# One load a stack from rows kept by row tile, and the first unit's maxima and shift in halves of its heads

## The chip, the cores and the metric

The kernel runs on one NeuronCore of a Trainium2 chip. Five engines work from their own instruction queues and meet at semaphores: TensorE (PE, matmuls), VectorE (DVE), ScalarE (ACT), GpSimd (POOL) and SyncE (SP, which only issues DMAs). The metric is the time of one execution on the device in microseconds (us).

## What is computed

Two layers over eight sequences of 512 tokens with 128 channels: an attention with 16 heads of 8 channels and a sliding window of 128 keys, then a block of causal attention and a top-2 mixture of eight experts. Each is followed by a residual sum and a layer norm.

```python
def attention(x, w_qkv, allowed):            # both layers, heads of 8 channels
    q, k, v = split(x @ w_qkv)               # [B, H, T, 8]
    scores = einsum('bhtd,bhsd->bhts', q, k) * 8 ** -0.5
    attn = softmax(where(allowed, scores, -inf))
    return merge(einsum('bhts,bhsd->bhtd', attn, v)) @ w_out

x = layernorm(x + attention(x, ..., (j <= i) & (j >= i - 128)))
h = layernorm(x, g1, b1)
r = x + attention(h, ..., j <= i)
f = layernorm(r, g2, b2)
out = sum over the two best experts e of gate_e * (gelu(f @ w1[e] + b1[e]) @ w2[e] + b2[e])
x = layernorm(x + out + r)
```

## The kernel before

**Units and iterations.** The attention work is cut into 16 units: unit u below 8 is sequence u in the local layer, unit 8 + b is sequence b in the causal layer. The main loop runs over iterations `it` from -2 to 15, each a row of steps k (6 in iteration -2, 14 for a local unit, 20 for a causal one). In iteration `it` the scores of unit `it` are made while the maxima of the units after it, the products with v of this one, and the last stages of the one before run beside them. Every engine walks through the same steps in a fixed order written out by hand (`MAXIMA`, `JOBS`, `project_at`); no planner moves anything. A queue that waits for a semaphore holds back all that stands behind it on its engine.

**Stacks.** The scores must be accurate although bf16 matmuls make them. So `project(u)` makes q and k in float32 in PSUM, and three bf16 parts are split off: the high part (`high_part`, L772, ScalarE), the rest (`split_rest`, L934, VectorE), the middle part (`middle_part`, L780, ScalarE) and the low part (`low_part`, L942, VectorE). SP stores these parts to a scratch in DRAM (`store`, L460), each into as many slots as it has factors in the product (three, two and one), and loads them back in another order (`load`, L467) as a stack: for each of two row tiles of 64 partitions, 48 rows of contraction (six slots of 8 channels), 8 heads and 512 tokens, so that one matmul over 48 rows sums all partial products. Row 48 and 49 of each half hold ones for k (`L447`, loaded once) and the shift for q (`load_shift`, L489).

**Maxima and shift.** Before the exponential the kernel needs a shift a query. `maxima(u, m)` (L1381) makes masked scores of 14 pieces of a local unit (20 of a causal one) on TensorE, L1402 the masks and L1411 the products; `maximum(u, m)` (L898, local L907 and L911) reduces each piece on VectorE. `split_shift` (L924) splits the negated maxima into two bf16 numbers, `turn_shift` (L1520) transposes them on TensorE, `take_shift` (L817) copies them on ScalarE, and `load_shift` puts them into rows 48 and 49 of q's stack by DMA. Then `scores(u, k)` (L1365) gives scores less the maximum in one matmul, and `exponent` (L737) takes the exponential.

**Order at the start.** Iteration -2 projects units 0 and 1. SP stores and loads unit 0, waits until that stack has landed (L475, since there is one scratch), then stores and loads unit 1. The maxima of unit 0 take steps 0 to 10 of iteration -1, the values job (`values`, L1481) stands at its step 1, and its shift follows; those of unit 1 begin at step 11 of iteration -1 and run on through steps 0 to 10 of iteration 0, one a step; unit 2's begin at step 11 of iteration 0. Unit 2 is projected at step 0 of iteration 0. PSUM buffers for scores, maxima, projections and turns come from a ring of three (`RING_AT`): each entry waits for the third one before it to be read.

## Time and profile before

| | |
|---|---|
| median of three runs | 786.75 us (780.80 to 787.21) |
| the profiled execution | 787.42 us, of which the span is 785.7 us |
| TensorE / VectorE / ScalarE / GpSimd busy | 81% / 73% / 59% / 54% of the span |
| first matmul of the maxima | 25.57 us |
| first score | 45.39 us |
| first score of unit 1 | 75.60 us |
| moved by DMA | 82.22 MB in 57549 packets |

A busy share is an average over stages with different limits: what a change in one stage is worth is read from the stage, not from the share. Starts are counted from the beginning of the span. "Landing" is when the data of a DMA is there and its semaphore is up; SP's row shows only the issue. The granted clock is TensorE's, as a share of 2.4 GHz.

### The profile page before, as it was taken

The page shows a single profiled execution, that of the slowest core. Times are in us where ns is not written, and L with a number is a line of the kernel's source. Part 1 is how long each engine was busy: PE and PEld are TensorE (multiplying, and loading weights), DVE is VectorE, ACT ScalarE, POOL GpSimd, SP SyncE. Part 2 cuts the span into 40 slices and gives each one's busy share as a digit, 9 for nine tenths or more (in the row PEclk, how much of TensorE's full clock was granted, in tenths as well). Part 3 has the DMA queues.
Part 4 walks back from the last instruction along what each step waited for, and adds up shares of the span by engine and source line. Part 5 has one row for each costly group of instructions (what it writes and reads, how often), then busy time and mean ns, then how long its engine had stood idle before and what let it go on. Part 6 is the DMA issues. An engine that isn't in the chain of part 4 may idle for free.

```text
span 785.7 us, 20471 instructions
## 1 busy us (share of the span) xinstructions
PE 635.7 (81%) x7679; PEld 390.0 (50%) x7679; DVE 577.1 (73%) x1308; ACT 460.8 (59%) x757; POOL 424.0 (54%) x643
## 2 busy tenths in 40 slices
PE   3578988989988788888879898988787997899850
PEld 1333544544444443444434343444337997899750
DVE  2555677777878989898889898988534775565676
ACT  2045665666766576767676767667663563555424
POOL 5026566567665444245546464656845555444663
PEclk8579999999999999999999999999979998999985
DMA  6744734744652625343535353510111223222505
GB/s 193 185 118 92 185 117 81 189 132 88 152 147 40 168 98 121 107 89 114 107 101 121 98 124 95 127 51 12 61 45 48 55 72 91 58 63 63 203 12 161
DMA packets 57549, 82.22 MB, mean 105 GB/s; under 512 B 7672, under 2 KB 48096, under 8 KB 54380
## 3 DMA queue, kind: packets, MB, share of 16 engines
q1 hardware_dynamic: 53132, 72.45, 35.9%
q0 software_dynamic: 4320, 8.47, 3.5%
q8 instruction: 62, 1.02, 0.6%
q14 instruction: 35, 0.29, 0.1%
HBM read 43.55 MB, written 37.17 MB: 103 GB/s over the span
## 4 chain that ended last, share of the span: by engine, by line
PE 43%; DVE 21%; DMA 9%; issue 9%; ACT 7%; POOL 4%; SPq 3%; another core or an unknown queue 1%; DVEq 0%; ACTq 0%; POOLq 0%
PE side_ps L1457 8%; PE pair_ps L1606 8%; PE pair_ps L1618 8%; DMA arena<-parts_dram 6%; PE pair_ps L1478 4%; PE pair_ps L1377 4%; DVE row_max L916 4%; ACT probs L745 4%; DVE row_max L918 3%; SPq L471 2%; DVE rest L939 2%; DMA arena<-shift_t 2%; PE side_ps L1517 2%; DVE row_max L921 2%; ACT parts L778 2%
## 5 line engine op out<-in xcount | busy, mean ns | idle before, releaser
L745 ACT ACTIVATE probs<-pair_ps 128x1024 f32<-128x1024 f32 x272 | 275.6, 1021 | 130.2 <-PE pair_ps L1377 123.0
L1457 PE MATMUL side_ps<-probs,v_aug 128*32 128x256 f32 (+3 forms) x2048 | 161.9, 411 | 7.8 <-POOL probs L650 3.0
L871 ACT ACTIVATE arena<-pair_ps,arena 128x128 f32<-128x128 f32 x284 | 80.9, 370 | 86.4 <-PE pair_ps L1606 55.5
L1377 PE MATMUL pair_ps<-arena 50*128 50x256 bf16 (+3 forms) x1024 | 107.7, 286 | 26.9 <-DMA arena<-shift_t 7.8
L637 POOL TENSOR_SCALAR_AFFINE_SELECT probs<-probs 128x512 f32<-128x512 f32 x96 | 61.4, 640 | 120.0 <-ACT probs L745 119.0
L703 POOL DMA_INDIRECT outputs_dram<-arena x71 | 70.6, 994 | 76.7 <-DVE arena L1262 55.3
L907 DVE TENSOR_REDUCE row_max<-pair_ps 128x4 f32<-128x768 f32 x96 | 89.0, 951 | 26.7 <-PE pair_ps L1411 26.1
L1606 PE MATMUL pair_ps<-arena 128*128 128x128 f32 x568 | 80.5, 287 | 21.7 <-DVE arena L1251 10.5
L1377 PEld LDWEIGHTS pair_ps<-arena 50*128 50x128 bf16 x1024 | 32.5, 95 | 108.5 <-issue 45.5
L1606 PEld LDWEIGHTS pair_ps<-arena 128*128 128x128 f32 x568 | 73.2, 201 | 24.6 <-issue 22.1
L916 DVE TENSOR_REDUCE row_max<-pair_ps 128x2 f32<-128x1024 f32 x64 | 76.5, 1219 | 7.4 <-PE pair_ps L1437 5.9
L1618 PE MATMUL pair_ps<-pack,arena 128*128 x568 | 78.8, 285 | 0.0
L1457 PEld LDWEIGHTS side_ps<-probs,v_aug 128*32 128x32 f32 x2048 | 47.9, 109 | 61.5 <-issue 35.3
L662 POOL DMA_INDIRECT rows_dram<-rows,row_at x64 | 63.9, 998 | 17.9 <-issue 15.4
L1618 PEld LDWEIGHTS pair_ps<-pack,arena 128*128 128x128 f32 x568 | 73.0, 201 | 0.1
L918 DVE TENSOR_REDUCE row_max<-pair_ps 128x2 f32<-128x768 f32 x64 | 60.9, 952 | 6.5 <-PE pair_ps L1437 6.4
L1431 PE MATMUL pair_ps<-first_b,eye_b 64*128 64x128 bf16 (+2 forms) x640 | 48.4, 229 | 20.2 <-ACT probs L745 9.7
L1437 PE MATMUL pair_ps<-arena 48*128 48x384 bf16 (+3 forms) x512 | 61.5, 297 | 0.0
L639 POOL TENSOR_SCALAR_AFFINE_SELECT probs<-probs 128x512 f32<-128x512 f32 x96 | 61.2, 637 | 0.0
L1260 DVE TENSOR_TENSOR arena<-pair_ps,pack 128x128 f32<-128x128 f32 x71 | 20.5, 289 | 48.6 <-PE pair_ps L1618 22.6
L648 POOL TENSOR_SCALAR_AFFINE_SELECT probs<-probs 128x256 f32<-128x256 f32 x64 | 26.7, 416 | 53.1 <-ACT probs L745 51.8
L1402 PE MATMUL pair_ps<-window_b,ident_b 64*64 64x256 bf16 x384 | 30.8, 311 | 30.1 <-DMA arena<-parts_dram 20.2
(177 smaller groups left out, 1049.9 us busy)
## 6 DMA issues: line engine op xcount, KB each, us to landing
arena<-parts_dram SPq DMA_DIRECT2D x96, 192.0 KB
parts_dram<-parts SPq DMA_DIRECT2D x32, 384.0 KB
parts_dram<-parts SPq DMA_DIRECT2D x32, 256.0 KB
pack<-in_pack SPq DMA_DIRECT2D x8, 578.0 KB
arena<-rows_dram SPq DMA_DIRECT2D x71, 65.0 KB
parts_dram<-parts SPq DMA_DIRECT2D x32, 128.0 KB
arena<-parts_dram SPq DMA_DIRECT2D x32, 128.0 KB
x_t<-in_x_t SPq DMA_DIRECT2D x8, 256.0 KB, 9.3
```

The source lines that it names most:

```text
L662: nc.gpsimd.indirect_dma_start(out=table[:, :], out_offset=bass.IndirectOffsetOnAxis(ap=row_at[:, j:j + 1], axis=0), in_=rows[:, j // NT, ...
L703: nc.gpsimd.indirect_dma_start(out=outputs[:, :], out_offset=bass.IndirectOffsetOnAxis(ap=place, axis=0), in_=block_y[n % Y_DEPTH], in_off ...
L745: nc.scalar.activation(probs[:, n % PROBS, :], pair_ps[RING_AT["score", n][0]][:, :, :].rearrange("p b t -> p (b t)"), ACT.Exp, scale=SCAL ...
L871: last = nc.scalar.activation(hidden[n % H_DEPTH][:, f * BLK:(f + 1) * BLK], hidden_ps[n % 2][:, f * BLK:(f + 1) * BLK], ACT.Gelu_apprx_ta ...
L907: nc.vector.tensor_reduce(top[:, i, :, 2 * g:2 * g + 2], pair[:, :, 0:2 * WIN].rearrange("p b (s k) -> p b s k", k=WIN), AX_X, ALU.max).th ...
L916: nc.vector.tensor_reduce(top[:, 3, :, 2 * g + m], pair[:, :, :], AX_X, ALU.max).then_inc(max_done, 1)
L918: nc.vector.tensor_reduce(top[:, 2, :, 2 * g + m - 2], pair[:, :, 0:3 * P], AX_X, ALU.max)
L1377: last = nc.tensor.matmul(pair[:, r, col:col + width], k_st[u % STACKS][own, gs, j * P:(j + 1) * P], q_st[u % STACKS][own, gs, q0:q0 + wid ...
L1437: last = nc.tensor.matmul(pair[:, r, col:col + keys], qs[own, gs, i * P:(i + 1) * P], ks[own, gs, 0:keys], start=False, stop=(n == len(wor ...
L1457: last = nc.tensor.matmul(o_ps[c * VHEAD:(c + 1) * VHEAD, q0:q0 + width], v_aug[u % 2][:, j, first:first + VHEAD], probs[:, slot, r * T + ...
L1606: last = nc.tensor.matmul(hidden_ps[n % 2][:, f * BLK:(f + 1) * BLK], block_w[n % W_DEPTH][:, PACK_W1 + f * P:PACK_W1 + (f + 1) * P], bloc ...
L1618: last = nc.tensor.matmul(y_ps[n % 2][:, 0:C], hidden[n % H_DEPTH][:, f * BLK:(f + 1) * BLK], pack[:, bass.ds(expert, 1), PACK_W2 + f * C: ...
```

## The change

It has four parts.

1. Columns by row tile: the columns of the q and k weights are ordered so that partitions 0 to 63 of every part belong to row tile 0 and 64 to 127 to row tile 1. The scratch has eight slots of 8 rows instead of six for each row tile (two of them filled with ones once, from `ones_b`), and two buffers, for even and odd units. Each part is stored in four DMAs (side, row tile) instead of two; each stack is loaded by two DMAs, one a side, of 112 partitions with the ones between the halves, instead of ten. All stores of a unit must land before its loads, where the high part's rows could go ahead of the others.
2. Unit 0 in halves of the heads: its stack is loaded in two halves, the order of the 14 maxima is changed (`local_maximum`) so that the first seven belong to heads 0 to 3 of each row tile, and there are two shifts, each split, turned, taken and loaded on its own (`split_half`, `turn_half`, `take_half`; these DMAs are issued by ScalarE). The first half's shift comes at steps 7 and 8 of iteration -1, the second's at step 3 of iteration 0. Maxima 7 to 10 stand at steps 9 to 12 of iteration -1, and 11 to 13 at steps 0 to 2 of iteration 0.
3. Unit 1's parts and rest have buffers of their own (in `resid`, which is not yet in use), so that its conversion and its stores need not wait for unit 0's. Its stack is loaded once the first half shift is in. Its 14 maxima all stand in iteration 0, two a step at steps 4 to 10.
4. The values job of unit 0 moves from iteration -1 to iteration -2, step 2.

```diff
-SLOTS = 6
+SLOTS = HALF // HD
 Q_SLOTS = (slice(0, 3), slice(4, 6), slice(3, 4))
 K_SLOTS = (slice(2, 5), slice(1, 6, 4), slice(0, 1))
-HIGH_ROWS = ((0, 24), (16, 40))
-LOW_ROWS = (((24, 48),), ((0, 16), (40, 48)))
...
-STACK_LOADS = 5 * TILES_R * 16
+STACK_ROWS = HALF + STACK_K
+STACK_STORES = 2 * PARTS * TILES_R * 16
+STACK_LOADS = 2 * 16
 SHIFT_LOADS = 2 * 16
+ONES_LOADS = (4 + STACKS) * 16
...
+        if u < 2:
+            for m in range(PAIRS[LOCAL]):
+                slot = (0, 4 + m // 2) if u else (-1, m) if m < 7 else (-1, m + 2) if m < 11 else (0, m - 11)
+                table.setdefault(slot, []).append((u, m))
+            continue
...
+def local_maximum(m):
+
+    half, j = m // 7, m % 7
+    if j < 6:
+        g = 2 * half + j % 2
+        return j // 2 + 1, [2 * g, 2 * g + 1]
+    return 0, [4 * half + n for n in range(4)]
...
+HALF_TURNS = {(-1, 8): 0, (0, 3): 1}
+HALF_SPLITS = {(-1, 7): 0, (0, 3): 1}
...
+        if (name, u) in (("shift", 0), ("v", 0)):
+            continue
         if real(u) and (name not in ("xt", "xf", "logits", "rank") or layer(u) == CAUSAL):
             out.append((name, u))
+    if (it, k) == (-2, 2):
+        out.append(("v", 0))
+    if (it, k) in HALF_TURNS:
+        out.append(("half", HALF_TURNS[it, k]))
...
+        second_unit = resid[:, :, :, :].rearrange("p b t c -> p (b t c)")
...
+        second_parts = second_unit[:, 0:PARTS * T].bitcast(BF16).rearrange("p (n s t) -> p n s t", n=PARTS, s=2)
+        second_rest = second_unit[:, PARTS * T:(PARTS + 2) * T].rearrange("p (s t) -> p s t", s=2)
+
+        def parts_of(u):
+            return second_parts if u == 1 else parts
+
+        def rest_of(u):
+            return second_rest if u == 1 else rest
...
-        scratch = nc.dram_tensor("parts_dram", (2, SLOTS, P, T), BF16, kind="Internal").ap()
+        scratch = nc.dram_tensor("parts_dram", (2, 2, TILES_R, SLOTS, HALF, T), BF16, kind="Internal").ap()
...
+        def stack_rows(buffer, side):
+            return scratch[buffer, side].rearrange("r s (d g) t -> (r s d) (g t)", g=GS)
...
+            for buffer in range(2):
+                for side in range(2):
+                    between = stack_rows(buffer, side)[STACK_K:HALF, :].rearrange("p (g t) -> p g t", t=T)
+                    sp.dma_start(between, ones_b[:, :].unsqueeze(1).to_broadcast(between.shape)).then_inc(ones_in, 16)
             for stack in k_st:
-                for r in range(TILES_R):
-                    sp.dma_start(stack[HALF * r + STACK_K:HALF * r + SCORE_K, :, :], ones_b[:, :]).then_inc(ones_in, 16)
+                sp.dma_start(stack[HALF + STACK_K:HALF + SCORE_K, :, :], ones_b[:, :]).then_inc(ones_in, 16)
...
-                        place = scratch[side, slots[part]].rearrange("s p t -> p s t")
-                        sp.dma_start(place, parts[:, part, side, :].unsqueeze(1).to_broadcast(place.shape)
-                                     ).then_inc(stored_low if part else stored_high, 16)
-
-                def load(side, first, last):
-                    stack = (q_st, k_st)[side][u % STACKS]
-                    by_row = scratch[side].rearrange("s (d r g) t -> (s d) r (g t)", d=HD, r=TILES_R)
-                    for r in range(TILES_R):
-                        sp.dma_start(stack[HALF * r + first:HALF * r + last, :, :].rearrange("p g t -> p (g t)"), by_row[first:last, r, :]
-                                     ).then_inc(stack_in[u % STACKS], 16)
-
-                if u:
-                    sp.wait_ge(stack_in[(u - 1) % STACKS], ((u - 1) // STACKS + 1) * STACK_LOADS)
+                        for r in range(TILES_R):
+                            place = scratch[u % 2, side, r, slots[part]].rearrange("s p t -> p s t")
+                            sp.dma_start(place, parts_of(u)[HALF * r:HALF * (r + 1), part, side, :].unsqueeze(1).to_broadcast(place.shape)
+                                         ).then_inc(stored, 16)
+
+                if u >= 2:
+                    sp.wait_ge(stack_in[(u - 2) % STACKS], ((u - 2) // STACKS + 1) * STACK_LOADS)
                 store(0, high_ready)
                 store(1, middle_ready)
                 store(2, low_ready)
                 if u >= STACKS:
                     sp.wait_ge(score_filled, BEFORE[u - STACKS + 1])
-                sp.wait_ge(stored_high, (u + 1) * 32)
-                for side in range(2):
-                    load(side, *HIGH_ROWS[side])
-                sp.wait_ge(stored_low, (u + 1) * 64)
-                for side in range(2):
-                    for rows_of_part in LOW_ROWS[side]:
-                        load(side, *rows_of_part)
+                sp.wait_ge(stored, (u + 1) * STACK_STORES)
+                if u == 0:
+                    sp.wait_ge(ones_in, ONES_LOADS)
+                    for half, landed in enumerate((first_heads_in, stack_in[0])):
+                        heads = slice(half * GS // 2, (half + 1) * GS // 2)
+                        for side, stack in enumerate((q_st[0], k_st[0])):
+                            sp.dma_start(stack[0:STACK_ROWS, heads, :].rearrange("p g t -> p (g t)"),
+                                         stack_rows(0, side)[0:STACK_ROWS, heads.start * T:heads.stop * T]).then_inc(landed, 16)
+                    return
+                if u == 1:
+                    load_x_t(2)
+                    sp.wait_ge(half_in[0], SHIFT_LOADS)
+                for side, stack in enumerate((q_st[u % STACKS], k_st[u % STACKS])):
+                    sp.dma_start(stack[0:STACK_ROWS, :, :].rearrange("p g t -> p (g t)"), stack_rows(u % 2, side)[0:STACK_ROWS, :]
+                                 ).then_inc(stack_in[u % STACKS], 16)
...
-                if real(it + 3) and it + 3 >= 2 and layer(it + 3) == LOCAL:
+                if it >= 0 and real(it + 3) and layer(it + 3) == LOCAL:
...
-                if real(it + 1):
+                if real(it + 1) and it + 1 > 0:
...
             def high_part(u):
 
                 act.wait_ge(projected, u + 1)
-                if u:
-                    act.wait_ge(stored_high, u * 32)
-                    act.wait_ge(stored_low, u * 64)
-                nc.scalar.activation(parts[:, 0, :, :], pair_ps[RING_AT["project", u][0]][:, :, :], ACT.Copy).then_inc(high_ready, 1)
+                if u >= 2:
+                    act.wait_ge(stored, u * STACK_STORES)
...
+            def take_half(half):
+
+                act.wait_ge(misc_filled, JOB["half", half])
+                nc.scalar.activation(first_shift_t[half][:, :], misc[0:2 * GS, :], ACT.Copy).then_inc(misc_taken, 1)
+                act.wait_ge(misc_taken, JOB["half", half])
+                for r in range(TILES_R):
+                    act.dma_start(q_st[0][HALF * r + STACK_K:HALF * r + SCORE_K, half * GS // 2:(half + 1) * GS // 2, :],
+                                  first_shift_t[half][GS * r:GS * (r + 1), :]).then_inc(half_in[half], 16)
...
+            def split_half(half):
+
+                tops = row_max[0][:, :, :, half * GS // 2:(half + 1) * GS // 2]
+                dve.wait_ge(max_done, 7 * (half + 1))
+                nc.vector.tensor_scalar(first_shift[:, half, :, :, 0, :], tops, -1.0, None, ALU.mult).then_inc(half_hi, 1)
+                dve.wait_ge(half_hi, half + 1)
+                nc.vector.scalar_tensor_tensor(out=first_shift[:, half, :, :, 1, :], in0=tops, scalar=-1.0,
+                                               in1=first_shift[:, half, :, :, 0, :], op0=ALU.mult, op1=ALU.subtract).then_inc(half_lo, 1)
...
+                if u == 0 and k % 7 == 0:
+                    pe.wait_ge(half_in[k // 7], SHIFT_LOADS)
+                    pe.wait_ge(ones_in, ONES_LOADS)
+                if u and k == 0:
+                    pe.wait_ge(shift_in[u % STACKS], shift_loaded(u))
...
+                if u == 0 and m == 0:
+                    pe.wait_ge(first_heads_in, STACK_LOADS)
+                if m == (0 if u else 7):
...
+            def turn_half(half):
+
+                pe.wait_ge(half_lo, half + 1)
+                for t in range(NT):
+                    last = nc.tensor.matmul(misc[0:2 * GS, t * P:(t + 1) * P],
+                                            first_shift[:, half, t, :, :, :].rearrange("p r s g -> p (r s g)"), ident_b[:, :],
+                                            start=True, stop=True)
...
-                    if it == -1 and ("shift", 0) in jobs_at(it, k):
-                        pe.wait_ge(misc_taken, JOB["shift", 0] - 1)
-                        turn_shift(0)
...
+                        if name == "half":
+                            turn_half(u)
...
-    columns = [head(gs, r) * HD + d for d in range(HD) for r in range(TILES_R) for gs in range(GS)]
+    columns = [head(gs, r) * HD + d for r in range(TILES_R) for d in range(HD) for gs in range(GS)]
```

## Rows read from the trace of the kernel before

**Rows 1.** The page: span, and the engines' shares of the chain that ended last.
```profile
span 785.7 us, 20471 instructions
...
PE 43%; DVE 21%; DMA 9%; issue 9%; ACT 7%; POOL 4%; SPq 3%; another core or an unknown queue 1%; DVEq 0%; ACTq 0%; POOLq 0%
```

**Rows 2.** Busy time by stretch; last three columns: granted clock, DMA share, GB/s.
```profile
13.00:25.50 12.50, 0.00 (x0) 0.00 (x0) 2.45 (x2) 2.08 (x2) 0.00 (x0) 0.50 0.72 166
25.50:45.40 19.90, 13.34 (x234) 9.44 (x234) 14.61 (x18) 1.18 (x2) 0.00 (x0) 0.59 0.72 175
45.40:75.60 30.20, 24.40 (x370) 11.22 (x370) 17.64 (x20) 17.34 (x19) 15.75 (x25) 0.86 0.52 124
```

**Rows 3.** Waits of TensorE: total us, times, longest us.
```profile
PE pair_ps L1402 <- DMA arena<-parts_dram: 20.2, 4, 15.1
...
PE pair_ps L1431 <- DMA arena<-parts_dram: 1.2, 1, 1.2
```

**Rows 4.** Timeline of SP's queue: start us, us of the group's issues.
```profile
8.86 4.43 SPq L464 DMA_DIRECT2D parts_dram<-parts  x6
...
25.55 4.21 SPq L464 DMA_DIRECT2D parts_dram<-parts  x6
...
42.46 1.29 SPq L492 DMA_DIRECT2D arena<-shift_t  x2
51.76 4.39 SPq L464 DMA_DIRECT2D parts_dram<-parts  x6
...
80.00 4.67 SPq L464 DMA_DIRECT2D parts_dram<-parts  x6
...
194.05 4.38 SPq L464 DMA_DIRECT2D parts_dram<-parts  x6
```

**Rows 5.** The chain in order of time, 0 to 50 us: start us, us, what.
```profile
12.84 2.23 DMA parts_dram<-parts
```

**Rows 6.** Stretches of 1 us, columns as in rows 2: the rate is the last.
```profile
4.00:5.00 1.00, 0.98 (x1) 0.49 (x2) 0.00 (x0) 0.00 (x0) 0.94 (x4) 1.00 0.93 350
...
12.00:13.00 1.00, 0.00 (x0) 0.00 (x0) 0.44 (x1) 0.00 (x0) 0.00 (x0) 1.00 1.00 333
...
58.00:59.00 1.00, 1.00 (x28) 0.47 (x24) 0.69 (x1) 0.73 (x2) 0.59 (x1) 1.00 0.76 205
59.00:60.00 1.00, 1.00 (x24) 0.48 (x28) 0.96 (x1) 0.72 (x2) 0.93 (x3) 1.00 0.80 188
...
95.00:96.00 1.00, 1.00 (x32) 0.63 (x28) 0.95 (x2) 0.75 (x1) 0.14 (x1) 1.00 0.81 98
```

**Rows 7.** Timeline of the start: start us, us, engine, line, operation, idle before.
```profile
25.57 0.43 PE L1402 MATMUL pair_ps<-window_b,ident_b 64*64 64x256 bf16 x4 [15.08 <-DMA arena<-parts_dram]
...
29.59 8.74 DVE L907 TENSOR_REDUCE row_max<-pair_ps 128x4 f32<-128x768 f32 x10 [1.40 <-PE pair_ps L1411]
...
40.62 0.20 DVE L929 TENSOR_SCALAR shift<-row_max 128x64 bf16<-128x64 f32 x1
...
45.39 0.61 PE L1377 MATMUL pair_ps<-arena 50*128 50x256 bf16 x4 [0.34 <-DMA arena<-shift_t]
```

**Rows 8.** Timeline of TensorE in iterations 0, 1 and 5.
```profile
56.89 0.39 PE L1377 MATMUL pair_ps<-arena 50*128 50x256 bf16 x4
...
58.18 0.39 PE L1377 MATMUL pair_ps<-arena 50*128 50x256 bf16 x4
58.50 0.30 PE L1402 MATMUL pair_ps<-window_b,ident_b 64*64 64x256 bf16 x4
...
58.90 0.64 PE L1457 MATMUL side_ps<-probs,v_aug 128*32 128x256 f32 x8
...
70.37 0.30 PE L1402 MATMUL pair_ps<-window_b,ident_b 64*64 64x256 bf16 x4 [3.52 <-DMA arena<-parts_dram]
...
99.53 0.30 PE L1402 MATMUL pair_ps<-window_b,ident_b 64*64 64x256 bf16 x4
...
212.41 0.30 PE L1402 MATMUL pair_ps<-window_b,ident_b 64*64 64x256 bf16 x4 [0.18 <-DMA arena<-parts_dram]
```

63 lines of the change are left out of this document (34 added, 29 removed).

## The prediction, made before the kernel was run

> **What bounds the kernel now.** I read the page first: a span of 785.7 us whose chain belongs to no single engine, TensorE with 43%, VectorE with 21%, DMA with only 9% [rows 1]. So I looked for where that DMA share sits. The busy times by stretch answer it: from 13 to 25.5 us TensorE, ScalarE and VectorE do next to nothing while the DMA engines are 72% busy, and the granted clock is at its lower level (0.50 of full, 1.2 GHz) [rows 2]. The waits of TensorE give the sizes: it waited 20.2 us in four waits for the stacks to land, one of 15.1 us, and 1.2 us more in unit 8 [rows 3]. The queue of SP shows the order that makes these waits: stores of unit 0 from 8.86 us, its loads behind them, and the stores of unit 1 only at 25.55 us, when unit 0's stack has landed, although the numbers were ready long before; from 51.76 us it is unit 2's turn, and from then on a store group stands in each iteration [rows 4]. The chain of waits has the last store of unit 0 landing at 12.84 + 2.23 = 15.07 us [rows 5]; the first maxima start at 25.57 us [rows 7]. The reader is to see three things: a start-up of 45.39 us before the first score [rows 7], one wait of 3.52 us for unit 2's stack at 70.37 us, and after that iterations in which the stack lands just in time (0.18 us of waiting at 212.41 us) [rows 8]. There the mixed work of TensorE, ScalarE and VectorE sets the pace, and this change takes none of that work away.
>
> **The rates of the transfers.** Stores from all 128 partitions run at 333 GB/s in a full microsecond (I use 340, since the share is full there), loads into 128 partitions at 350; the stack loads of 24 partitions run at 188 to 205, and their tail, loads of 16 and 8 partitions, at 98 [rows 6]. A unit's stores are 2 x (384 + 256 + 128) KB = 1.573 MB, 4.6 us at 340 GB/s; from first issue to landing they took 15.07 - 8.86 = 6.2 us, so 1.6 us are fixed. A last issue needs 2.2 us to land [rows 5].
>
> **Part 1: stores split by row tile.** The same bytes now leave in 12 transfers of 64 partitions. No row shows 64 partitions. The bounds are 170 GB/s (half of 340: the same rate for each partition) and 340. I take 205, the highest rate that any transfer on fewer than 128 partitions shows [rows 6]: 1.573 / 0.205 = 7.7 us instead of 4.6. Up to four more issues stand ahead of the last, which started at 12.84 us; at half of the 4.21 / 6 = 0.70 us that one took in unit 1 [rows 4] it starts at 14.2 us, so even at the full rate the stores land no earlier than 14.2 + 2.2 = 16.4 us. The Trainium skill speaks against this part. SBUF — State Buffer, section "Door 1: The DMA port swizzle", says that partitions 0 to 63 reach only 8 of the 16 DMA ports, for which it gives about 218 GB/s, and by DMA: Bandwidth & Descriptors, "Rules for kernel authors", two transfers on the two halves run one behind the other. By it the stores would take 7.2 us, half a microsecond less than I count; no row here shows such a transfer.
>
> **Part 2: one load a stack.** Two loads of 112 partitions replace ten, and carry 2 x 112 x 8 KB = 1.835 MB instead of 1.573 (the rows of ones between the halves come along). Bounds: 188 GB/s, as the 24-partition loads (9.8 us), and 350 (5.2 us). The nearest row is that of 128 partitions; scaled by 112/128 it is 306 GB/s, so 6.0 us. Stores and loads of one unit then need 1.6 + 7.7 + 2.2 + 6.0 = 17.5 us from the first issue. Before it is 70.37 - 51.76 = 18.6 us and 212.41 - 194.05 = 18.4 us, and unit 3 may take 99.53 - 80.00 = 19.5 us before anyone waits [rows 4, 8]. So later iterations stay covered, with 0.9 to 2 us to spare. The waits of 0.2 and 1.2 us in units 7 and 8 go: -1.4 us. The clearing of the ones costs at the start: four DMAs of 128 KB from 16 partitions at 98 GB/s are 5.4 us behind the weights, of which I let 1.0 us delay the first stores (bounds 0 and 2.5; they are issued from 2.7 us on, and the weights fill the queues to about 5).
>
> **Part 3: halves of the heads.** Unit 0's stores land at 8.86 + 1.0 + 1.6 + 7.7 = 19.2 us. The first heads (0.917 MB) need 2.2 + 3.0 us: 24.4 us, against 25.57 [rows 7]. Seven maxima at 8.74 / 10 = 0.87 us each, with 1.1 us for the first fill and the longer seventh tile, are 7.2 us: 31.6 us. Before, fourteen maxima and the values matmuls between them (now in the idle time after the projections, where nothing waits for TensorE) took 40.62 - 25.57 = 15.05 us. From the shift to the first score it was 45.39 - 40.62 = 4.8 us; with 0.5 us for sharing the DMA engines with unit 1's stores the first score stands at 36.9 us: 8.5 us earlier. The second heads land by 27.4 us, covered by the first seven maxima. ScalarE, which now issues the shift's two DMAs, has nothing queued behind them in iteration -1.
>
> **Part 4: iteration 0 pays back.** It gets maxima 11 to 13 of unit 0 and all 14 of unit 1, where it had 11 of unit 1: six more. A step with one of each is 58.18 - 56.89 = 1.29 us, of which one maximum is 58.90 - 58.50 = 0.40 us on TensorE [rows 8]; with two it is 1.69 us there, and 1.74 us on VectorE; I take 1.8 us. Seven steps: 7 x 0.51 + 0.3 (two long tiles) = 3.9 us. The turn of the second half's shift stands at step 3 behind VectorE, which still has maximum 13 and the split to do (an estimate of 0.7 us from its 0.87 us a maximum, bounds 0 and 1.5). The activation and two DMA issues (1.29 / 2 = 0.65 us each [rows 4]) stand on ScalarE ahead of the exponential of step 4, for whose PSUM buffer the scores of step 5 wait: 1.2 us (bounds 0 and 1.9). Against this the 3.52 us stall goes. The iteration was 75.6 - 45.4 = 30.2 us [rows 2]; it becomes 30.2 - 3.5 + 3.9 + 0.7 + 1.2 = 32.5 us and ends at 69.4 us: 6.2 us earlier than before.
>
> **Part 5: unit 1's own buffers.** They cost nothing themselves: unit 1's conversions run in idle time of ScalarE and VectorE, and its stores queue behind unit 0's loads. They end at 27.4 + 7.7 = 35.1 us; x_t of unit 2 comes behind them just in time for its projection at 38 us; the loads, held back until the first shift is in (36.9 us), land at 36.9 + 2.2 + 6.0 = 45.1 us, wanted at step 4, which stood 56.89 - 45.39 = 11.5 us behind the first score: 49.1 us. Unit 2's stores start 51.76 - 45.39 = 6.4 us after the first score, at 43.3 us, and its stack lands 17.5 us later, at 60.8 us; wanted at 36.9 + (70.37 - 3.52 - 45.39) + 5.8 = 64.2 us. If that cover of 3.4 us is gone, the wait comes back one for one.
>
> **The sum.** 6.2 + 1.4 = 7.6 us. The profiled execution took 787.42 us: 779.8. The median of the runs is 0.67 us lower: 779.
>
> **Rivals.**
> (B) The half-partition stores are not slower. Then they land at 16.4 us, 2.8 us earlier, with loads at 350 GB/s 0.4 us more, and if the 1.2 us on ScalarE is hidden, the gain is 12 us: 775. For it: nothing here shows 64 partitions to be slow. Against: all partial transfers shown are.
> (C) Iteration 0 gives it back. The clock was at the lower level in most of 25.5 to 45.4 us (mean 0.59) and partly in iteration 0 (0.86) [rows 2]. If it stays at 1.2 GHz while two maxima a step are due, TensorE's 1.69 us become 2.4 to 3.4 (four mask matmuls take 0.43 us instead of 0.30 [rows 7, 8]), +0.6 to +1.6 us a step, up to 11 us: 783 to 788. Against: the mean of 0.86 holds the stall, and at 58 us the mask matmuls are the short ones, behind the long projection, which still stands there.
> (D) The other side: the load of 112 partitions gets no more than the 24-partition rate, 188 GB/s. A unit then needs 1.6 + 7.7 + 2.2 + 9.8 = 21.3 us, against 18.4 to 19.5 available, and TensorE waits 2 to 3 us in each of six iterations (about 16 us), plus 3 us at the start: 779 + 19 = 798. It decides from a load time of 7.0 to 8.0 us on, which is below 230 to 260 GB/s.
> **Chances.** Forecast 0.45 (776 to 783), B 0.22 (772 to 777), C 0.20 (783 to 788), D 0.13 (790 to 803). The bounds of the unknowns within the forecast (stores, ones, step length) are 3 us either way. A measurement of this kernel tells about 1% (7.9 us) from no change; the forecast lies on that line, so half of it counts as faster: 0.22 + 0.22 = 0.44 faster, 0.43 the same, 0.13 slower. The range 771 to 788 leaves out D.
>
> **What would show it.** Right: first maxima at 24 to 25 us, first score near 37, unit 1's next iteration near 69, windows of some 205 GB/s in stores and over 290 in stack loads, and no wait for arena<-parts_dram from iteration 0 on. Wrong: windows at 340 in the stores (B); granted clock of 0.5 in iteration 0 beyond the projection (C); waits of 2 us or more for the stacks in iterations 1 to 6 (D).

## The result, and the profile after

The changed kernel took 796.38 us (median of four runs, 788.0 to 802.04) where the kernel before took 786.39 beside it: a ratio of 1.0092 with an interval of 1.005 to 1.0135 (one disturbed run, of 802.04, is in the median and not in the ratio). Two more measurements of the same kernel, on two other occasions, gave 1.0052 (1.0016 to 1.0087) and 1.0079 (1.0036 to 1.0122). So it is slower by 0.5 to 0.9%, 4 to 7 us, where 7.6 us of gain were forecast. All ratios below are to the kernel before, run in turns with the variant on the same chip. Between measurements the times differ: before itself took 765.43 us in one and 786 to 790 in the others, and the cause isn't known (one of the others has the same chip number). So total times are compared within one measurement only.

The start-up came out nearly as forecast (24.4 us for the first maxima and 36.9 for the first score). The timeline of TensorE in the profile after (start us, us, engine, line, operation, idle before it):

```profile
25.27 0.43 PE L1474 MATMUL pair_ps<-window_b,ident_b 64*64 64x256 bf16 x4 [13.57 <-DMA arena<-parts_dram]
...
33.07 0.58 PE L1604 MATMUL side_ps<-ident_b,first_shift 128*16 128x128 bf16 x4 [2.33 <-DVE first_shift L997]
...
37.53 0.61 PE L1446 MATMUL pair_ps<-arena 50*128 50x256 bf16 x4 [1.38 <-DMA arena<-first_shift_t]
...
49.40 0.38 PE L1604 MATMUL side_ps<-ident_b,first_shift 128*16 128x128 bf16 x4 [2.18 <-DVE first_shift L997]
...
52.95 0.61 PE L1446 MATMUL pair_ps<-arena 50*128 50x256 bf16 x4 [1.27 <-ACT probs L795]
...
72.22 0.39 PE L1446 MATMUL pair_ps<-arena 50*128 50x256 bf16 x4 [1.09 <-DMA arena<-shift_t]
```

Read it as three marks: the first maxima at 25.27 us and the first score at 37.53 us, 7.9 us earlier than before's 45.39 [rows 7], and unit 1's first score at 72.22 us, only 3.4 us earlier than the 75.60 at which before's iteration 0 ended [rows 2]. In between stand a wait for VectorE at the second half's turn (2.18 us) and one for ScalarE (1.27 us).

From the next iteration on TensorE waits for the stacks. The same timeline, iterations 1, 2, 4 and 5:

```profile
97.57 0.30 PE L1474 MATMUL pair_ps<-window_b,ident_b 64*64 64x256 bf16 x4 [2.77 <-DMA arena<-parts_dram]
...
127.78 0.30 PE L1474 MATMUL pair_ps<-window_b,ident_b 64*64 64x256 bf16 x4 [1.04 <-DMA arena<-parts_dram]
...
183.97 0.30 PE L1474 MATMUL pair_ps<-window_b,ident_b 64*64 64x256 bf16 x4 [1.13 <-DMA arena<-parts_dram]
...
213.74 0.30 PE L1474 MATMUL pair_ps<-window_b,ident_b 64*64 64x256 bf16 x4 [0.62 <-DMA arena<-parts_dram]
```

Before had no wait at unit 3's stack (99.53 us) and 0.18 us at 212.41 us [rows 8]. Behind these four stands one of 1.1 us in the iteration of unit 6, so 6.7 us in all. The queue of SP shows where they come from (start us, us of the group's issues):

```profile
9.22 8.01 SPq L514 DMA_DIRECT2D parts_dram<-parts  x12
18.69 1.76 SPq L530 DMA_DIRECT2D arena<-parts_dram  x4
20.50 8.46 SPq L514 DMA_DIRECT2D parts_dram<-resid  x12
...
69.15 1.40 SPq L543 DMA_DIRECT2D arena<-shift_t  x2
76.62 8.84 SPq L514 DMA_DIRECT2D parts_dram<-parts  x12
86.98 0.81 SPq L537 DMA_DIRECT2D arena<-parts_dram  x2
```

Twelve stores keep SP issuing for 8 to 8.8 us, where six took 4.2 to 4.7 [rows 4]. Unit 3's stack goes out from 76.62 us and is there at 97.57 us: 21.0 us, of which 10.4 pass before the loads can be issued and 10.6 behind that. The chain of waits of the start, in order of time, shows one of these stores, the last one's landing, and the load of the first heads:

```profile
9.93 0.62 SPq L514
...
16.63 2.04 DMA parts_dram<-parts
...
19.10 6.13 DMA arena<-parts_dram
```

And the busy times by stretch (columns as in [rows 2]: the last three are granted clock, DMA share, GB/s), unit 3's stores and its loads, then two microseconds in iteration 0:

```profile
76.60:87.00 10.40, 9.01 (x152) 5.20 (x144) 8.46 (x9) 7.38 (x10) 5.96 (x10) 1.00 0.59 154
87.00:97.60 10.60, 7.43 (x140) 3.97 (x138) 6.48 (x8) 6.39 (x7) 7.34 (x12) 1.00 0.79 224
...
50.00:51.00 1.00, 1.00 (x30) 0.69 (x32) 0.44 (x1) 0.40 (x1) 0.00 (x0) 0.94 0.88 203
51.00:52.00 1.00, 0.68 (x8) 0.00 (x0) 1.00 (x2) 0.13 (x1) 0.00 (x0) 0.50 0.56 136
```

While the stores are issued the DMA engines are only 59% busy, which speaks against bytes as what holds the stores up. In the other pair the granted clock drops to 0.50, the 1.2 GHz level, less than two microseconds behind the half-turn's wait, which ended at 49.40 us, and it stays there until 57.6 us.

The theory from this: each store of 64 partitions costs SP about 0.65 us whatever it carries, so a unit's stores take 4 us more than before (10.4 us against 6.2); the larger loads give back less than expected; and the stack then sets the pace of the local iterations. The rivals: the halves of the heads give back in iteration 0 whatever they bring (C); or the loss lies elsewhere, in the later units.

### The profile page after: what moved, and what is told of

Read it like the earlier page. It is cut to its first block, busy times and chain, and to the rows that moved or that the text cites. A ratio compares the mean times of both kernels' runs of the same rounds, so it can differ in the third digit from the quotient of the medians.

```text
span 786.2 us, 20454 instructions
## 1 busy us (share of the span) xinstructions
PE 633.6 (81%) x7683; PEld 385.7 (49%) x7683; DVE 576.3 (73%) x1310; ACT 461.5 (59%) x758; POOL 422.7 (54%) x643
## 4 chain that ended last, share of the span: by engine, by line
PE 39%; DVE 19%; DMA 12%; issue 9%; ACT 7%; SPq 5%; POOL 5%; another core or an unknown queue 2%; ACTq 0%; DVEq 0%; POOLq 0%
PE pair_ps L1686 8%; PE pair_ps L1698 7%; PE side_ps L1529 7%; DMA arena<-parts_dram 7%; SPq L514 4%; PE pair_ps L1550 4%; PE pair_ps L1446 3%; DVE row_max L973 3%; ACT probs L795 3%; POOL rows_dram L712 2%; DVE row_max L975 2%; DMA rows_dram<-rows,row_at 2%; DMA arena<-shift_t 2%; DVE row_max L978 2%
## 5 line engine op out<-in xcount | busy, mean ns | idle before, releaser
L967 DVE TENSOR_REDUCE row_max<-pair_ps 128x4 f32<-128x768 f32 (+1 forms) x112 | 108.8, 990 | 37.3 <-PE pair_ps L1483 36.6
L1686 PE MATMUL pair_ps<-arena 128*128 128x128 f32 x568 | 78.9, 283 | 22.6 <-DVE arena L1319 11.4
L1686 PEld LDWEIGHTS pair_ps<-arena 128*128 128x128 f32 x568 | 71.4, 197 | 26.6 <-issue 23.9
L1529 PEld LDWEIGHTS side_ps<-probs,v_aug 128*32 128x32 f32 x2048 | 47.9, 110 | 62.7 <-issue 34.7
L1698 PE MATMUL pair_ps<-pack,arena 128*128 x568 | 76.5, 279 | 0.0
L712 POOL DMA_INDIRECT rows_dram<-rows,row_at x64 | 63.8, 996 | 18.2 <-issue 15.7
L1698 PEld LDWEIGHTS pair_ps<-pack,arena 128*128 128x128 f32 x568 | 70.7, 196 | 0.1
L1503 PE MATMUL pair_ps<-first_b,eye_b 64*128 64x128 bf16 (+2 forms) x640 | 49.3, 232 | 19.2 <-ACT probs L795 8.4
L1005 DVE TENSOR_TENSOR rest<-pair_ps,parts 128x1024 f32<-128x1024 f32 x15 | 18.4, 1224 | 43.5 <-ACT parts L827 43.5
## 6 DMA issues: line engine op xcount, KB each, us to landing
pack<-in_pack SPq DMA_DIRECT2D x8, 578.0 KB, 10.4
```

What stands on the lines that cost most here:

```text
L712: nc.gpsimd.indirect_dma_start(out=table[:, :], out_offset=bass.IndirectOffsetOnAxis(ap=row_at[:, j:j + 1], axis=0), in_=rows[:, j // NT, ...
L967: nc.vector.tensor_reduce(top[:, i, :, heads[0]:heads[-1] + 1], pair[:, :, 0:len(heads) * keys].rearrange("p b (s k) -> p b s k", k=keys), ...
L1529: last = nc.tensor.matmul(o_ps[c * VHEAD:(c + 1) * VHEAD, q0:q0 + width], v_aug[u % 2][:, j, first:first + VHEAD], probs[:, slot, r * T + ...
L1686: last = nc.tensor.matmul(hidden_ps[n % 2][:, f * BLK:(f + 1) * BLK], block_w[n % W_DEPTH][:, PACK_W1 + f * P:PACK_W1 + (f + 1) * P], bloc ...
L1698: last = nc.tensor.matmul(y_ps[n % 2][:, 0:C], hidden[n % H_DEPTH][:, f * BLK:(f + 1) * BLK], pack[:, bass.ds(expert, 1), PACK_W2 + f * C: ...
```

## The experiments

"Part 1" in this section is part 1 of the change, columns, stores and loads, which the prediction costs in its parts 1 and 2; "the rest" is what its parts 3 to 5 cost.

**after_again, before_again and after_third: how much is chance.** No edit; the changed kernel twice more, the kernel before once.

> The changed kernel once more, beside the others on one chip. Its first profile had the first score at 37.5 us (before: 45.4), unit 1's first score at 72.2 (before: 75.6), and had lost that lead by unit 6 (218.7 against 217.2); then it lost 3.5 us more in the causal iterations, in which three stretches of granted clock at 0.5 stand where before has one, and won 4.7 us back behind 560 us, where before has five such stretches and it has three. If the waits for the stacks are the cause (theory 1), the lead is lost by unit 6 again, at the same places. If the causal loss belongs to the change, it is there again at 2 to 4 us; if it is chance in where the clock falls (theory 2), these stretches stand elsewhere and the loss is not the same. Time against before: 1.00 to 1.015.

> The kernel before, once more, for where its clock falls. In its first profile the clock is low in one stretch of 3.4 us between 250 and 555 us, in four other kernels in three to four stretches of 10 to 17 us. If that belongs to the kernel, this profile has one or none there and the causal part (first shift at 278.8 us to the last at 548.4) takes 269 to 270 us again; if it is chance, there are two to four stretches and it takes 271 to 273 us.

> The changed kernel beside both: 1.005 to 1.01 of before, with 5 to 9 us of waits of TensorE for the stacks of units 3 to 8, which the two others don't have. Parts 1 and 2's transfers then cost 1.5 to 2% together on the same chip. If the causal units make the difference instead (by chance of the clock), the waits don't explain it and the ratio moves by more than 0.5% from its first measurement.

Measured: 1.0052 and 1.0079 as above, and for before once more 787.94 us with a span of 786.2. The table takes two marks from SP's queue in each trace, the issue of unit 1's shift and that of unit 7's (the end of the local iterations that the change touches), with the waits for stacks between the two:

| profile | unit 1's shift | unit 7's shift | between | stack waits between | unit 7's shift to the end |
|---|---|---|---|---|---|
| before | 72.6 | 243.2 | 170.5 | 1.4 | 542.5 |
| before_again | 73.0 | 243.3 | 170.4 | 1.4 | 542.9 |
| after | 69.2 | 244.8 | 175.6 | 6.7 | 541.4 |
| after_again | 69.2 | 249.0 | 179.8 | 9.2 | 544.2 |
| after_third | 67.7 | 245.9 | 178.2 | 10.0 | 542.4 |

Two things follow. The lead of 3.4 to 4.9 us at unit 1 is there in each of the three and is lost in each by unit 7: the stretch between is 5.1, 9.3 and 7.7 us longer than in before, and its waits for stacks are 5.3, 7.8 and 8.6 us more, so the waits account for the loss within 1.5 us. And behind unit 7 the kernels are alike within the 3 us by which the same kernel differs from itself, so the later units, which also have the new transfers but whose stacks nobody waits for, are not the cause. The first profile did lose some 3 us in the causal iterations (272.6 us from unit 8's shift to unit 15's, against 269.6), but before_again takes 273.6 us for them, after_again 273.7 and after_third 271.4, so that is chance. The mean of the three spans is 789.2, 3.3 us above the mean of before's two, where the ratios say 4 to 7. Two of the three profiled executions, of 788.0 and 790.09 us, were the fastest of their measurements, whose medians are 796.38 and 796.63: by chance the profiles show short executions of the changed kernel.

**transfers: the disputed cost by itself.** A program with the transfers of both kernels and nothing else; the whole computation is left out. Each kind is run three times, each group waited for before the next.

```diff
+for copies in (3, 2, 1):   # one transfer at a time: from 128 partitions, then from 64
+    place = wide[0, 0:copies].rearrange("s p t -> p s t")
+    place = halves[0, 0, 0:copies].rearrange("s q t -> q s t")
+# then a unit's six stores, a unit's twelve, and its loads: 2 of 112, 4 of 48, 8 of 24, 2 of 128
```

> A kernel that leaves the computation out (it copies the input to the output) and measures transfers, each awaited before the next. In this order, three times each: one store from 128 partitions in 3, 2 and 1 copies of 1 KB a partition; the same from 64 partitions; the six stores of a unit from 128 partitions; its twelve stores from 64; two loads of 112 partitions with 8 KB each; four of 48; eight of 24; two of 128. Theory 1 (the issue bounds): a store of 64 partitions keeps the queue of SP busy for 0.6 us or more whether it carries one copy or three, one of 128 partitions 0.35 us, and the twelve land in 9.5 to 10.5 us where the six land in 6.2. Rival (half the partitions move at half the rate, and SP only waits for the DMA engines behind it): single stores of 64 partitions are issued as fast as those of 128, and 0.60 us is seen only in the group of twelve. Loads: four of 48 partitions land in 11.8 us as in the kernel (1.573 MB, 170 GB/s), two of 112 in 8.6 to 9.0, eight of 24 in the same time as four of 48 (10.5 to 12), two of 128 in 8 to 9.

Measured; the chain of waits first, a single store of three copies from 128 partitions (393 KB), from 64 partitions (197 KB), and two neighbours in a group of twelve:

```profile
36.11 2.51 DMA wide_dram<-parts
...
55.24 2.63 DMA halves_dram<-parts
...
94.04 0.61 SPq L77
94.69 0.61 SPq L77
```

Then SP's queue (groups of three rounds each; a round is a third of the distance to the next group's start):

```profile
76.04 16.20 SPq L69 DMA_DIRECT2D wide_dram<-parts  x18
94.04 26.80 SPq L77 DMA_DIRECT2D halves_dram<-parts  x36
122.31 18.54 SPq L82 DMA_DIRECT2D stack<-halves_dram  x6
149.32 25.00 SPq L88 DMA_DIRECT2D stack<-wide_dram  x12
184.56 24.41 SPq L95 DMA_DIRECT2D stack<-wide_dram  x24
216.59 15.27 SPq L101 DMA_DIRECT2D stack<-halves_dram  x6
```

In this single store half the bytes from 64 partitions take as long as the whole from 128. The rival, that a lone store of 64 partitions is issued as fast as one of 128, falls: its issue takes 0.58 us with three copies and 0.47 to 0.48 with one, where 128 partitions take 0.33 to 0.36. In a row of six the issues of 128 partitions are longer, 0.38 to 1.06 us. A unit's stores take 18.0/3 = 6.0 us in six (as before's 6.2 us) and 28.3/3 = 9.4 us in twelve. Loads: 2 of 112 partitions 9.0 us, 4 of 48 partitions 11.7, 8 of 24 partitions 10.7, and 2 of 128, which carry 14% more bytes than the 112, 7.3. The 128-partition loads are faster than was expected (8 to 9 us). A unit alone thus needs 9.4 + 9.0 = 18.4 us; the forecast had 17.5 with all else running.

**two_queues: bytes or issues.** Again transfers alone, the computation left out: twelve stores as above, twelve with one copy each (half of the unit's bytes), and six from SP beside six from ScalarE.

```diff
+twelve(sp, (0, 1), (3, 2, 1), landed)
+twelve(sp, (0, 1), (1, 1, 1), landed)
+twelve(sp, (0,), (3, 2, 1), landed)          # with twelve(act, (1,), (3, 2, 1), act_landed)
+for rows_in in (112, 96, 128):               # two loads each
```

> Transfers without the computation again (the input is copied to the output). Three times each: the twelve stores of 64 partitions from SP; the same twelve with one copy each (half the bytes, as many issues); the twelve with six issued by SP and six by ScalarE at the same time; two loads of 112, of 96 and of 128 partitions. Theory 1 (issues bound): twelve 9.4 us; one copy each 9.0 to 9.4; two queues 6 to 7. Rival (the DMA engines move half the partitions at 180 GB/s, as the single stores of 64 do: 2.64, 2.33 and 1.91 us for 3, 2 and 1 copies): one copy each 6 to 7 us by bytes if the issues were free, two queues 9 or more. Loads: 9.0 us for 112, 7.3 for 128, and for 96 between 7 and 8.5.

Measured, from the chain of waits: the end of the last round of twelve with one copy, and ScalarE's issues beside SP's:

```profile
88.17 0.60 SPq L42
...
89.19 1.90 DMA halves_dram<-parts
91.11 0.66 ACTq L42
91.79 1.03 ACTq L42
92.85 1.77 ACTq L42
```

With half the bytes each issue but the first still takes 0.60 us, and the rounds take 8.9, 8.9 and 9.2 us, against 9.3 in the same program with all the bytes. So the number of issues sets the time of the twelve stores and not the bytes: this is what tells the theory from a limit by bytes. Two queues don't help much, and less than was expected (6 to 7 us): the round is 8.5 us, ScalarE's issues stretch to 0.65 to 1.8 us, and SP's six take 6.4 us. What the two queues share is not shown. The rates of single transfers do depend on the partitions: from 128 partitions the third copy adds 0.39 us to the second (2.51 and 2.12) for 131 KB, 336 GB/s; from 64 it adds 0.31 for 66 KB, 211 GB/s (the second adds 0.42 us to the first, of which 0.10 is a longer issue). The Trainium skill, SBUF — State Buffer, section "Door 1: The DMA port swizzle", gives about 218 GB/s for one half of the partitions, and the traces agree at 211; but it is not what bound the stores here.

**part1_only: part 1 and the large loads in the kernel before.**

```diff
-STACK_LOADS = 5 * TILES_R * 16
+STACK_STORES = 2 * PARTS * TILES_R * 16
+STACK_LOADS = 2 * 16
...
-                        place = scratch[side, slots[part]].rearrange("s p t -> p s t")
+                        for r in range(TILES_R):
+                            place = scratch[u % 2, side, r, slots[part]].rearrange("s p t -> p s t")
```

> The kernel before with part 1 alone: columns by row tile, 12 stores and two loads a unit, ones between the halves; start and order as before. Theory 1: slower than before, because each local iteration waits 1 to 3 us for its stack and iteration 0 some 5 us, 1.01 to 1.02 of before, with the stack landing 19 to 21 us behind the first store. Rival 2 (the loss is in the new order of iteration 0): the same as before within 0.3%.

Measured: 804.93 us, a ratio of 1.0214 (1.016 to 1.0268), some 17 us slower. The waits of TensorE (total, times, longest):

```profile
PE pair_ps L1400 <- DMA arena<-parts_dram: 31.9, 7, 17.2
...
PE pair_ps L1429 <- DMA arena<-parts_dram: 3.3, 1, 3.3
```

Against 20.2 in four and 1.2 us [rows 3] that is 13.8 us more. In this kernel SP still waits for a unit's stack before it stores the next one, so a later stack also delays the next unit's stores. Unit 1's wait is 2.53 us, unit 2's 5.65 (3.52 before), unit 3's 2.62. Unit 7's shift is issued at 259.6 us, 16.5 us behind before's.

**parts_2_to_4: the rest of the change, with before's columns and transfers** (part 1 of the change undone; the label counts the remaining parts).

```diff
-STACK_LOADS = 2 * 16
+STACK_LOADS = 5 * TILES_R * 16
...
-    columns = [head(gs, r) * HD + d for r in range(TILES_R) for d in range(HD) for gs in range(GS)]
+    columns = [head(gs, r) * HD + d for d in range(HD) for r in range(TILES_R) for gs in range(GS)]
```

> The rest of the change without part 1 and without the large loads: columns, stores of 128 partitions and loads of 24, 16 and 8 partitions as before; halves of the heads, the turn of the second half's shift at step 3 and unit 1's own buffers as after. If the transfers of parts 1 and 2 cost the time (theory), this is faster than before by 0.8 to 1.3%: first maxima near 20.5 us, first score near 32.8, no wait of TensorE for a stack from unit 2 on above 0.5 us, and a wait near 2 us at the half's turn. If iteration 0 gives back what the halves bring whatever the transfers are (rival C), its time is within 0.3% of before's.

Measured: 780.25 us against 790.3, a ratio of 0.9885 (0.9817 to 0.9953). SP's queue:

```profile
71.91 4.38 SPq L512 DMA_DIRECT2D parts_dram<-parts  x6
76.38 4.22 SPq L525 DMA_DIRECT2D arena<-parts_dram  x10
```

Here the loads of the high rows are issued at 76.38 us, 4.5 us behind the first store and while the later stores are still under way, against 10.4 us from first store to first load after the change. Unit 3's stack lands unnoticed. TensorE:

```profile
21.07 0.43 PE L1491 MATMUL pair_ps<-window_b,ident_b 64*64 64x256 bf16 x4 [9.97 <-DMA arena<-parts_dram]
...
33.35 0.61 PE L1463 MATMUL pair_ps<-arena 50*128 50x256 bf16 x4 [1.40 <-DMA arena<-first_shift_t]
...
45.23 0.38 PE L1621 MATMUL side_ps<-ident_b,first_shift 128*16 128x128 bf16 x4 [2.23 <-DVE first_shift L1014]
...
145.26 0.30 PE L1491 MATMUL pair_ps<-window_b,ident_b 64*64 64x256 bf16 x4 [0.28 <-DMA arena<-parts_dram]
```

The first score stands at 33.35 us, unit 7's shift at 233.0, and between unit 1's shift (64.5) and unit 7's the only wait for a stack is 0.28 us. Rival C falls as the cause of the slowdown: the wait at the half's turn (2.23 us) and seven microseconds at the lower clock behind it (46.5 to 53.3 us) are there, and the gain remains. after_third, measured beside this run, is at 1.0079: what differs between the two is the transfers and the order of the columns. With part1_only and after_third this makes a table of four: before 1, part 1 alone 1.021, the rest alone 0.989, both 1.005 to 1.009. The two parts nearly add up, 17 - 9 = 8 us against 4 to 7 measured.

**wide_stores and four_loads: the same question with four loads.** wide_stores is the change with the columns and the six stores of before, but four loads of 48 partitions; four_loads is before with these four in place of its ten.

```diff
-STACK_LOADS = 5 * TILES_R * 16
+STACK_LOADS = 2 * TILES_R * 16
...
-                sp.wait_ge(stored_high, (u + 1) * 32)
-                for side in range(2):
-                    load(side, *HIGH_ROWS[side])
+                    load(side, 0, STACK_K)
```

> The changed kernel with the columns as before, so that each part is stored from all 128 partitions in two DMAs (6 a unit, not 12), and each stack is loaded in four DMAs of 48 partitions; buffers, halves of the heads and order as in the changed kernel. Theory 1 (SP's issues bound the stores: 0.65 us for each store of 64 partitions, whatever its size): the stores of a unit take some 6.2 us from first issue to landing instead of 10.4, the stack lands in 15 to 17 us, TensorE does not wait for a stack from iteration 0 on, the lead of the start is kept, and the time is 0.98 to 0.99 of before. Rival 1 (the loads are the slow part, 10.6 us in the changed kernel against 8.2 forecast): with 48 partitions at a time they are no faster, the stack lands after 17 us or more and most of the waits stay; 0.99 to 1.00. Rival 2 (iteration 0 and the clock are the loss, not the DMAs): no better than the changed kernel.

> The kernel before with one edit: four loads of 48 partitions a unit instead of ten of 8 to 24, issued when all stores are in. If transfers into more partitions are faster, the stack lands in 14 to 16 us from the first store instead of 18.4, the first maxima start at 22 to 23.5 us instead of 25.6, unit 1's and unit 2's stacks come 2 to 3 us earlier each, and the time is 0.990 to 0.995 of before. If the 24-partition loads were bound by something else (rival), nothing moves: 1.000.

Measured: wide_stores 0.9999 (0.9965 to 1.0033), four_loads 1.0062 (1.0026 to 1.0097). Both miss their theories, 0.98 to 0.99 and 0.990 to 0.995. Fewer loads that start later are worse than ten: in four_loads the first stack's loads take from 15.90 to 27.87 us, 12.0 us, where before's ten took from 13.33 to 25.57, 12.2 us, with the earlier start. The ten with their early start are worth 0.6% in before, and 1.1% with the halves of the heads (parts_2_to_4 against wide_stores, in two measurements). In wide_stores the loads are the slow part, as its rival 1 had it. SP's queue and TensorE at unit 4's stack, the worst one:

```profile
102.70 5.06 SPq L510 DMA_DIRECT2D parts_dram<-parts  x6
110.24 1.72 SPq L534 DMA_DIRECT2D arena<-parts_dram  x4
...
123.28 0.58 PE L1471 MATMUL pair_ps<-window_b,ident_b 64*64 64x256 bf16 x4 [2.42 <-DMA arena<-parts_dram]
```

The loads take 13.0 us here, and the stack 20.6 us from its first store, although the stores are few. But such waits are rarer than in the changed kernel: 3.3 us in all from unit 1's shift to unit 7's, against 9.2 us in after_again beside it.

**after_late and wide_late: the second half's turn a step later.** after_late is the changed kernel with this edit, wide_late is wide_stores with it.

```diff
-HALF_TURNS = {(-1, 8): 0, (0, 3): 1}
+HALF_TURNS = {(-1, 8): 0, (0, 4): 1}
```

> The changed kernel with the turn of the second half's shift at step 4 instead of step 3 of iteration 0, nothing else. Theory C: no wait of 2.2 us at 47 us, no fall of the clock at 51 to 57.6 us, unit 1's first score at 68 to 70 us instead of 72.2; the waits for the stacks in iterations 1 to 6 then grow by part of what is won, since the stacks of units 3 to 7 land no faster: 1.000 to 1.004 of before against 1.005.

> The kernel with stores from 128 partitions (wide_stores), and the turn of the second half's shift one step later (step 4 of iteration 0). In wide_stores TensorE waits 2.2 us for that turn at 43.0 us, the granted clock falls to 0.5 from 45 to 58.7 us, and its steps take 2.75 us instead of 1.8. If that wait brings the clock down (theory C), the clock stays at 1.0 there, unit 1's first score comes at 65 to 67 us instead of 70.8, and the time is 0.990 to 0.996 of before. Rival: the clock falls anyway, because TensorE waits for VectorE in each step with two maxima; then unit 1's first score stays at 69 to 71 us and nothing is won. A second rival: the half shift lands too late for step 7, and the wait stands there.

Measured: after_late 1.0057 (1.0017 to 1.0096), wide_late 0.9943 (0.9926 to 0.9961). In both the 2.2 us of waiting and the low clock of iteration 0 go, and unit 1's shift is issued 3.6 and 4.0 us earlier. But after_late misses its range (1.000 to 1.004): it gives back part of this at the next stack already:

```profile
94.93 0.43 PE L1474 MATMUL pair_ps<-window_b,ident_b 64*64 64x256 bf16 x4 [3.77 <-DMA arena<-parts_dram]
```

The wait for unit 3's stack is 3.77 us, 1.0 longer than in the changed kernel, and by unit 7 (247.3 us) nothing is left. With these transfers the stack sets the pace, so what is saved elsewhere in these iterations is waited for again. The two runs stand side by side in one measurement and differ in nothing but the transfers and the columns: 1.0057 against 0.9943.

**full_load: 128 partitions instead of 112.** after_late with the ones of rows 112 to 127 written and loaded too.

```diff
-STACK_ROWS = HALF + STACK_K
+STACK_ROWS = P
...
-ONES_LOADS = (4 + STACKS) * 16
+ONES_LOADS = 8 * 16
```

> after_late with loads of all 128 partitions instead of 112 (rows 112 to 127 of the scratch are ones too; the three small loads of ones into k's stacks go, four more DMAs of 128 KB fill the scratch at the start). Measured by themselves, two loads of 112 partitions land in 9.0 us and two of 128, with 14% more bytes, in 7.3. If the same holds here, a stack lands 18.5 to 19.5 us behind its first store instead of 20 to 21, the waits of iterations 1 to 6 (10.8 us in after_late) fall below 4 us, and the time is 0.996 to 1.001 of before. Rival: the transfers of x_t and x_tok behind the loads hold them up in either form, and nothing moves: 1.003 to 1.008. The longer filling may delay the first stores by 1 to 2 us and take part of it back.

Measured: 761.32 us against 765.43, a ratio of 0.994 (0.9914 to 0.9967). The eight transfers of ones hold the first stores up to 12.29 us, so the first score stands at 41.88 us. SP's queue and TensorE at unit 3's stack:

```profile
87.69 0.81 SPq L536 DMA_DIRECT2D arena<-parts_dram  x2
...
96.67 0.30 PE L1473 MATMUL pair_ps<-window_b,ident_b 64*64 64x256 bf16 x4 [1.51 <-DMA arena<-parts_dram]
```

The loads take 9.0 us where those of 112 partitions took 10.6, with the same twelve stores ahead of them (10.7 us). Unit 3's stack takes 19.7 us, only 3.1 us of stack waits are left (1.51, 0.93 and 0.65 us) of after_late's 10.8, and unit 7's shift is issued at 239.9 us. (The kernel of wide_ten issues that shift at 234.0 us in this measurement and at 234.5 in another, where it takes 27 us longer as a whole, so these early marks can be compared.) So the twelve stores alone don't make the slowdown: with faster loads behind them it is gone. This is the changed kernel's scheme at its best in these runs, and still behind the ten loads.

**wide_ten and wide_ten_again: the fastest.** parts_2_to_4 with the turn at step 4.

```diff
-HALF_TURNS = {(-1, 8): 0, (0, 3): 1}
+HALF_TURNS = {(-1, 8): 0, (0, 4): 1}
```

> wide_late with the ten loads of before (24, 16 and 8 partitions, the high part's rows issued as soon as its stores are in) instead of four of 48. Measured by themselves, eight loads of 24 land in 10.7 us and four of 48 in 11.75, and the first ones run beside the last stores. Expected: the first maxima at 19.5 to 20.5 us instead of 21.1, the waits at 45, 62 and 119 us (1.9, 1.6, 2.1) gone or under 1 us, unit 1's first score 1 to 3 us earlier than 66.8, time 0.990 to 0.994 of before against 0.9943. Rival: 28 more issues of SP in the start delay unit 1's stores, and nothing is won.

> The fastest variant again, on one chip with the changed kernel: 0.985 to 0.990 of before if it was no matter of the other chip; 0.3 to 0.5% faster than the same with the turn at step 3, if moving the turn is worth a wait of 2 us and one stretch at the lower clock.

Measured: 754.88 us against 765.43, 0.9859 (0.9833 to 0.9884), and in another measurement 782.22 against 790.3, 0.9891 (0.9819 to 0.9963). It beats both kernels by over 1%. That is more than wide_ten's forecast of 0.990 to 0.994, but not by its reasoning: unit 1's first score, expected 1 to 3 us before wide_late's 66.8, comes at 70.32 us. And the later turn brings nothing over parts_2_to_4 (0.9885), where 0.3 to 0.5% were expected. The timeline of wide_ten_again says why:

```profile
44.50 0.43 PE L1491 MATMUL pair_ps<-window_b,ident_b 64*64 64x256 bf16 x4 [1.83 <-DMA arena<-parts_dram]
...
56.13 0.61 PE L1463 MATMUL pair_ps<-arena 50*128 50x256 bf16 x4 [2.99 <-DMA arena<-first_shift_t]
```

The wait at the turn is gone, but the shift itself is now late for the score of step 7 (2.99 us), and unit 1's stack for its first maxima (1.83 us). From unit 1's shift on it has no wait for a stack at all, and its local iterations are 27.4 to 27.5 us apart five times in a row; the sixth, in which the maxima of the first causal unit begin, takes 28.9. That is what the iterations take when no stack is late, 166.2 us for the six.

## Why the prediction was wrong

| step | forecast | measured |
|---|---|---|
| first store issued | 9.9 us | 9.22 |
| unit 0's stores landed | 19.2 | 18.67 |
| first maxima | 24.4 | 25.27 |
| seven maxima | 7.2 us | 7.25 |
| first score | 36.9 | 37.53 |
| iteration 0 | 32.5 us | 34.7 |
| unit 1's first score | 69.4 | 72.22 |
| unit 3's stack, first issue to landing | 17.5 us | 21.0 |
| stack waits in iterations 1 to 6 | none | 6.7 to 10.0 us |

**The start** was right to 0.9 us, partly by errors that cancel, which is luck: the first stores came 0.36 us later than before's and not 1.0 (before_again starts its own at 9.49 us, so even that may not be the ones), and the loads of the first heads took 6.5 us and not 5.2.

**The step that failed is "So later iterations stay covered", in part 2 of the prediction.** Its 17.5 us from a unit's first store to the landing of its stack measured 21.0, and TensorE wanted the stack after 97.57 - 2.77 - 76.62 = 18.2 us. The demand was nearly right: the 18.4 us taken from unit 7 hold 0.18 us of waiting [rows 8], so it too is 18.2. Both terms of the supply were too small.

- The stores, +1.1 us: 9.3 us forecast, 10.4 measured in iteration 1. I priced them by bytes at 205 GB/s and gave an extra issue 0.35 us, half of what a 128-partition issue takes. In the start-up the issues took 0.60 to 0.73 us: the last of the twelve goes out 16.63 - 9.22 = 7.4 us behind the first and lands 2.04 us later, 9.45 us in all. That this is so close to 9.3, and the landing at 18.67 us to 19.2, looked like a confirmation of 205 GB/s; it was luck, as two_queues shows: half the bytes take nearly as long. The prediction also counts "up to four more issues" ahead of the last, where there are six. Eleven at the 0.70 to 0.74 us of [rows 4] and 2.2 us to land are 9.9 to 10.3 us; with them the sum is 18.1 to 18.5 us, and next to nothing was left of the cover on paper.
- The loads, +2.4 us: 2.2 + 6.0 = 8.2 us forecast by scaling a 128-partition load by 112/128. Alone they take 9.0 us, so the scaling fails by 0.8 us; in iteration 1 they take 10.6. The rate over that stretch, 224 GB/s, is more than the stack's 1.835 MB in 10.6 us (173 GB/s), since x_t and x_tok of the next unit are issued right behind. That they cost the other 1.6 us is likely and was not tested.

Either error alone would have used up the 0.7 us between 17.5 and 18.2. This is rival D by its own condition: it "decides from a load time of 7.0 to 8.0 us on", and without the 2.2 us to land the measured one is 10.6 - 2.2 = 8.4. Its unit took 21.3 us by slow loads alone; the measured 21.0 us are reached by both terms. Its price of 16 us was too high (6.7 to 10.0 us of waits, and behind the one at 97.57 us the granted clock is at 0.50 for six microseconds), and that its total of 798 us lies so near the median of 796.38 is in part luck. Of the mark set for it, "waits of 2 us or more for the stacks in iterations 1 to 6", the first profile has one.

**Iteration 0** took 2.2 us more than the sum. The turn of the second half waits 2.18 us for VectorE, where I had 0.7 (bound 1.5); the wait for ScalarE was 1.27 us, forecast 1.2. A third wait has no term in the sum: 1.09 us for unit 1's own shift at its first score (72.22 us), where before has none at 75.60 us. The timeline of VectorE in the profile after shows what the 0.7 left out:

```profile
43.62 1.22 DVE L1005 TENSOR_TENSOR rest<-pair_ps,parts 128x1024 f32<-128x1024 f32 x1 [3.80 <-ACT parts L827]
...
45.97 1.23 DVE L1011 TENSOR_TENSOR parts<-rest,parts 128x1024 bf16<-128x1024 f32 x1 [0.26 <-ACT parts L832]
47.11 1.22 DVE L967 TENSOR_REDUCE row_max<-pair_ps 128x8 f32<-128x1024 f32 x1
48.36 0.29 DVE L995 TENSOR_SCALAR first_shift<-row_max 128x32 bf16<-128x32 f32 x1
48.69 0.56 DVE L997 SCALAR_TENSOR_TENSOR first_shift<-row_max,first_shift 128x32 bf16<-128x32 f32 x1
```

The conversion of unit 2's parts has two passes of 1.2 us on VectorE in steps 1 to 3, one of them right ahead of the last maximum, which is the long tile. Behind the first wait of TensorE the clock falls to 0.50 until 57.6 us, which is rival C's mechanism on a stretch of seven microseconds. after_late and wide_late show the price of the wait at the turn and the low clock together, 3.6 to 4.0 us.

**Parts 3 to 5 of the sum hold, and more comes of them,** when before's transfers carry them: parts_2_to_4 has the first score at 33.35 us (forecast 36.9) and unit 1's at 67.48 (forecast 69.4), although its iteration 0 takes 34.1 us too, and it is 10 us faster than before. What the forecast could have asked is what part 1 buys at all: the chain of the start has no row in which a store or load of before is held up by the order of its rows, while [rows 4] shows its six issues at 0.70 us each, and twice the issues cost twice that if issues and not bytes count.

**Open**: how the loss divides between the twelve stores and the two loads (full_load changes the loads, with their ones; no run changes the stores alone), and how much of the iterations' time beyond the waits is the clock. With its waits taken off the changed kernel needs 168.2 to 170.6 us from unit 1's shift to unit 7's, where wide_ten_again needs 166.2: 2.0 to 4.4 us. Before has 2.9 us of the same kind.
